# Query tile by query tile: the last attention group's evacuation and the closing steps of the last four tiles

## What is computed

```python
# L1 attention, H = 16 heads of Q/K width 8 and V width 32
Q = _split_heads(x, H)
K = _split_heads(x @ Wk + bk, H)
V = _split_heads(x @ Wv + bv, H)
scores = jnp.einsum('bhqd,bhkd->bhqk', Q, K) + mask      # causal
attn = jax.nn.softmax(scores, axis=-1)
o = jnp.einsum('bhqk,bhkd->bhqd', attn, V)
return x + jax.nn.gelu(o, approximate=False) @ Wf + bf
# L1 feed-forward
h = jax.nn.relu(jnp.einsum('bsd,dw->bsw', x, w1) + b1)
return jnp.einsum('bsw,wd->bsd', h, w2) + b2
# the layers, the last two of six
x = x + _L1_attn_ref(_layernorm(x, axis=-1), ...)
x = x + 0.5 * _L1_ffn_ref(_layernorm(x, axis=-1), ...)
```

## Time and profile before

| | us |
|---|---|
| median of 3 runs | 1076.71 |
| lowest, highest | 1074.05, 1086.48 |
| the profiled execution, its own time | 1089.29 |
| its span | 1087.5 |
| PE busy in it | 920.0 (85%) |
| DVE busy | 713.5 (66%) |
| ACT busy | 513.0 (47%) |
| mean granted PE clock | 0.948 of full speed |

### The profile page before, as it was taken

One profiled execution on the slowest core, in us unless ns is written; L12 is line 12 of the kernel. 1 busy time (PEld: TensorE's weight loads), 2 busy tenths in 40 slices (PEclk: granted clock), 3 DMA queues, 4 the chain that ended last, 5 costly groups with the idle time before them and its releaser, 6 DMA issues.

```text
span 1087.5 us, 19966 instructions
## 1 busy us (share of the span) xinstructions
PE 920.0 (85%) x7332; PEld 459.6 (42%) x7353; DVE 713.5 (66%) x1675; ACT 513.0 (47%) x884; POOL 257.8 (24%) x405
## 2 busy tenths in 40 slices
PE   2788888778888687798889899899899989999986
PEld 1444446565676466444323333233322223332225
DVE  7899953468876666775755588566488757676012
ACT  1133332234444232354565556656556656566772
POOL 1546420045554555421311001112000000000000
PEclk9999998999998887988999899999899999999997
DMA  5300000000000040041002300001500000000000
GB/s 183 67 14 1 1 0 1 1 1 1 1 2 1 1 79 10 2 81 20 23 11 58 54 8 24 2 12 35 74 2 11 12 1 15 7 10 5 12 2 10
DMA packets 30935, 23.20 MB, mean 21 GB/s; under 512 B 9609, under 2 KB 27897, under 8 KB 30840
## 3 DMA queue, kind: packets, MB, share of 16 engines
q1 hardware_dynamic: 29928, 21.39, 9.1%
q10 hardware_dynamic: 912, 0.54, 0.2%
HBM read 17.32 MB, written 4.34 MB: 20 GB/s over the span
## 4 chain that ended last, share of the span: by engine, by line
PE 61%; DVE 16%; ACT 7%; POOL 6%; issue 5%; DMA 3%; SPq 1%; ACTq 0%; DVEq 0%; POOLq 0%
PE psum L1677 11%; PE psum L1692 10%; PE psum L1653 7%; DVE arena L1290 5%; PE psum L1618 5%; PE psum L1565 3%; PE psum L1412 3%; PE psum L1371 2%; ACT arena L967 2%; PE psum L1576 2%; PE psum L1534 2%; PE psum L1422 2%; POOL rs L697 2%; DMA arena<-arena 2%; PE psum L1599 2%
## 5 line engine op out<-in xcount | busy, mean ns | idle before, releaser
L1290 DVE TENSOR_REDUCE arena<-psum 128x2 f32<-128x1024 f32 (+2 forms) x320 | 336.3, 1063 | 146.6 <-PE psum L1618 83.2
L967 ACT ACTIVATE arena<-psum 128x1024 f32<-128x1024 f32 (+3 forms) x320 | 286.7, 898 | 169.3 <-PE psum L1653 95.6
L697 POOL TENSOR_TENSOR rs<-ve,mhalf 128x1 f32<-128x1 f32 x128 | 70.7, 559 | 389.3 <-DVE ve L1084 388.8
L1677 PE MATMUL psum<-arena 128*32 128x512 f32 (+3 forms) x1280 | 153.2, 551 | 1.3 <-ACT arena L967 1.3
L1692 PE MATMUL psum<-arena,ones 128*32 128x512 f32 (+3 forms) x1280 | 153.7, 553 | 0.0
L1618 PE MATMUL psum<-arena 48*128 48x512 bf16 (+3 forms) x640 | 114.2, 358 | 25.9 <-ACT arena L967 13.8
L1653 PE MATMUL psum<-arena 50*128 50x512 bf16 (+3 forms) x640 | 116.8, 361 | 11.6 <-DMA arena<-arena 4.0
L1653 PEld LDWEIGHTS psum<-arena 50*128 50x128 bf16 x640 | 31.1, 93 | 200.8 <-issue 135.1
L936 ACT ACTIVATE rh<-psum,fb 128x128 f32<-128x128 f32 x128 | 36.5, 370 | 60.9 <-PE psum L1565 56.9
L803 POOL TENSOR_TENSOR arena<-arena 128x512 f32<-128x512 f32 x15 | 19.1, 1274 | 188.2 <-DMA arena<-scr_sums 188.2
L1371 PE MATMUL psum<-WguT,xqT 128*128 128x352 f32 x128 | 52.1, 536 | 7.0 <-DVE hb L1115 5.8
(11 more groups left out here) (186 smaller groups left out, 1494.9 us busy)
## 6 DMA issues: line engine op xcount, KB each, us to landing
arena<-scr_parts SPq DMA_DIRECT2D x96, 64.0 KB
arena<-scr_sums SPq DMA_DIRECT2D x60, 64.0 KB, 2.0
scr_parts<-arena SPq DMA_DIRECT2D x12, 256.0 KB, 2.6
arena<-arena SPq DMA_DIRECT2D x124, 2.0 KB, 1.7
X<-in_L_attn_src_dram SPq DMA_DIRECT2D x4, 256.0 KB, 4.9
out_dram<-X SPq DMA_DIRECT2D x16, 64.0 KB, 1.6
arena<-in_c_zsel_dram SPq DMA_DIRECT2D x1, 512.0 KB, 3.8
arena<-in_L_attn_Wk_dram SPq DMA_DIRECT2D x1, 512.0 KB
```

Of the source, the lines that this page charges most:

```text
L697: v.tensor_tensor(rs[:, u, t:t + 1], ve[:, u, t:t + 1], mhalf[:, :], ALU.pow).then_inc(s_rstd[u], 1)
L967: v.activation(pr[:, u % RING, pp, :, 0:CH - off], both(("scores", n))[0][:, :, off:CH], ACT.Exp).then_inc(s_p, 1)
L1290: v.tensor_reduce(MXP[:, j, 2 * pp:2 * pp + 2, m], both(("max", g, pp, j, m))[0][:, :, 0:hi - lo], AX_X, ALU.max).then_inc(s_mxd, 1)
L1677: last = mm(bank(O_BANK)[VD * h:VD * h + VD, off:CH], V[kb // TPC][:, kb % TPC, GH * (g % GPC) + h, :], pr[:, u % RING, h // 2, h % 2, 0:C ...
```

## The change

The last group (g = 15, `LAST`) no longer waits for its last cell. Behind diagonal cell 12+j no later cell adds to the columns of query tile j, so these 128 columns of both banks are final. `take_tile` copies them from bank 6 to `GT` on ACT, and `invert_tile` takes the reciprocal of the sums on DVE straight out of bank 7 into `DN` and multiplies. `take_o`, `take_d` and `invert_last` fall away for this group. Since PE goes on writing into the same two banks, `values` and `sums` of the next diagonal cell wait for the copy and for the reciprocal of the tile before (`s_otl`, `s_dtl`). Behind the cells, `gelu` moves from iteration end+3 to end+1, and the chains of the four tiles start one iteration apart where they stood side by side. The test for the last group in `gather_sums` goes, since it isn't called for it any more.

```diff
+        s_otl, s_dtl = sem("last_o_tile_copied"), sem("last_dn_tile_inverted")
...
                     put(end + 2, "store_inverse", g)
                     put(end + 3, "spread_inverse", g)
                     put(end + NORM_AT, "norm", g)
-                else:
-                    for j in range(TPC):
-                        put(end + 1 + j // 2, "invert_last", g, j)
                 if g % GPC == GPC - 1:
-                    put(end + (3 if last else GELU_AT), "gelu", c)
+                    put(end + (1 if last else GELU_AT), "gelu", c)
                     for j in range(TPC):
                         t = TPC * c + j
-                        put(end + (4 if last else GELU_AT + 1 + j), "wf", t)
-                        first = end + (5 if last else RELU_START + RELU_TILE * j)
+                        put(end + (1 if last else GELU_AT + 1) + j, "wf", t)
+                        first = end + (2 + j if last else RELU_START + RELU_TILE * j)
                         for k, name in enumerate(("f_stats", "d_norm", "d_turn", "d_hidden", "d_out", "d_add")):
                             put(first + k, name, 2 * TILES + t)
             out = [x for k in sorted(slots) if k < 0 for x in slots[k]]
...
                     if 0 < u <= len(CELLS):
                         out.append(("values" if i == 0 else "sums", u - 1))
                         g, kb = CELLS[u - 1]
-                        if kb == TPC * (g // GPC + 1) - 1:
+                        if g + 1 == MGROUPS and kb >= TPC * (CHUNKS - 1):
+                            out.append(("take_tile" if i == 0 else "invert_tile", kb % TPC))
+                        elif kb == TPC * (g // GPC + 1) - 1:
                             out.append(("take_o" if i == 0 else "take_d", g))
                     out += others[cut * i:cut * (i + 1)] + slots.get(2 * u + i, [])
 
...
                     act.wait_ge(s_wf, TPC * (c - 1))
                 v.copy(GT[c % 2][:, g % GPC, :], bank(O_BANK)).then_inc(s_ot, 1)
 
+            def take_tile(j):
+
+                q = slice(P * j, P * j + P)
+                act.wait_ge(s_av, GROUP_U[LAST] + TPC * (CHUNKS - 1) + j + 1)
+                if j == 0:
+                    act.wait_ge(s_wf, TPC * (CHUNKS - 2))
+                v.copy(GT[LAST // GPC % 2][:, LAST % GPC, q], bank(O_BANK)[:, q]).then_inc(s_otl, 1)
+
             def take_d(g):
                 act.wait_ge(s_dn, GROUP_U[g + 1])
                 if g >= 2:
...
                 dve.wait_ge(s_dg[g % 2], 16 * GH * (g // 2 + 1))
                 v.reciprocal(DG[g % 2], DG[g % 2]).then_inc(s_rd, 1)
 
-            def invert_last(g, j):
+            def invert_tile(j):
+
                 q = slice(P * j, P * j + P)
-                r = DN[g % 2][:, q]
-                o = GT[g // GPC % 2][:, g % GPC, q]
-                dve.wait_ge(s_dt, g + 1)
-                dve.wait_ge(s_ot, g + 1)
-                me.wait(me.did(v.reciprocal(r, r)))
+                r, o = DN[LAST % 2][:, q], GT[LAST // GPC % 2][:, LAST % GPC, q]
+                dve.wait_ge(s_dn, GROUP_U[LAST] + TPC * (CHUNKS - 1) + j + 1)
+                if j == 0:
+                    dve.wait_ge(s_on, LAST - 1)
+                v.reciprocal(r, bank(D_BANK)[:, q]).then_inc(s_dtl, 1)
+                dve.wait_ge(s_dtl, j + 1)
+                dve.wait_ge(s_otl, j + 1)
                 v.tensor_tensor(o, o, r, ALU.mult).then_inc(s_onl, 1)
 
             def add_wf(n):
...
                     pe.wait_ge(s_vc, TPC * (c + 1))
                 if kb == 0:
                     B[O_BANK].free(pe)
+                if g == LAST and kb > TPC * (CHUNKS - 1):
+                    pe.wait_ge(s_otl, kb - TPC * (CHUNKS - 1))
                 pe.wait_ge(s_p, GP * (u + 1))
                 for h in range(GH):
                     last = mm(bank(O_BANK)[VD * h:VD * h + VD, off:CH], V[kb // TPC][:, kb % TPC, GH * (g % GPC) + h, :],
...
                 end = kb == TPC * (c + 1) - 1
                 if kb == 0:
                     B[D_BANK].free(pe)
+                if g == LAST and kb > TPC * (CHUNKS - 1):
+                    pe.wait_ge(s_dtl, kb - TPC * (CHUNKS - 1))
                 for h in range(GH):
                     last = mm(bank(D_BANK)[VD * h:VD * h + VD, off:CH], ones1[:, 0:VD],
                               pr[:, u % RING, h // 2, h % 2, 0:CH - off], start=(kb == 0), stop=end,
```

More of the change, by code:

```diff
@@ L357, in build @@
         GROUP_U = [CELLS.index((g, 0)) for g in range(MGROUPS)] + [len(CELLS)]
+        LAST = MGROUPS - 1
         MAXES = [[(g, pp, j, m) for pp in range(GP) for j in range(TPC)
@@ L519, in build @@
         PLAN += causal(PLAN)
-        for kind in sorted({x[0] for x in PLAN} - {"quotients", "max", "invert_last"}):
+        for kind in sorted({x[0] for x in PLAN} - {"quotients", "max"}):
             counts = [x[1] for x in PLAN if x[0] == kind and len(x) == 2]
@@ L657, in gather_sums @@
             def gather_sums(g):
-                if g + 1 < MGROUPS:
-                    sp.wait_ge(s_dt, g + 1)
-                    w = GH * CH // P
-                    for h in range(GH):
-                        sp.dma_start(DG[g % 2][VD * h:VD * h + VD, :],
-                                     DN[g % 2][VD * h:VD * h + 1, :].rearrange("o (p n) -> o p n", n=w)
-                                     ).then_inc(s_dg[g % 2], 16)
+                sp.wait_ge(s_dt, g + 1)
+                w = GH * CH // P
+                for h in range(GH):
+                    sp.dma_start(DG[g % 2][VD * h:VD * h + VD, :],
+                                 DN[g % 2][VD * h:VD * h + 1, :].rearrange("o (p n) -> o p n", n=w)
+                                 ).then_inc(s_dg[g % 2], 16)
             def store_inverse(g):
@@ L1001, in _ @@
                    ff0=lambda g: gelu_ff(g, 0), ff1=lambda g: gelu_ff(g, 1), d_turn=d_copy, d_hidden=d_relu,
-                   e_turn=e_turn, e_k=e_k, e_v=e_v, scores=exponentials, take_o=take_o, take_d=take_d, gelu=gelu,
+                   e_turn=e_turn, e_k=e_k, e_v=e_v, scores=exponentials, take_o=take_o, take_tile=take_tile, take_d=take_d, gelu=gelu,
                    turn_max=max_copy)
@@ L1329, in _ @@
                    e_norm=e_norm, max=take_max, row_max=row_max,
-                   invert=invert, invert_last=invert_last, wf=add_wf)
+                   invert=invert, invert_tile=invert_tile, wf=add_wf)
         @block.tensor
```

## The result

Over 20 runs of each the median went from 1081.17 us (1070.11 to 1092.59) to **1072.85 us** (1064.69 to 1077.95). The ratio is 0.9947 [0.9923, 0.9970], which is 5.7 us faster; over all 20 runs of each the mean fell by 8.3 us, with a standard error of 1.5. The first figure is the smaller one because the ratio leaves out executions more than 1.5% above a kernel's fastest: 5 of 20 of before, none of after. The three differences of the means together are 7.85 +- 0.95 us.

The account below looks back on a forecast made before the run. PE bounds the chain; the last group's tail loses time to two pauses (4.29, 3.08 us) and half clock. Terms 2.2 + 7.0 + 1.3 = 10.5 us, taken as 10 off the 1076.71 median: 1066.7 us, range 1061 to 1074.

Parts of the forecast that it names:

- The likeliest case: Whole kernel: a gain of 8.5 to 11.5 us, the forecast itself, chance 0.50.
- the faster old tail: Rival: the old tail ran at full rate in other executions, so gain 4.7 us, time 1072; chance 0.15.
- within 1%: Whole kernel: outcome less than 1% (10.8 us) either way, chance 0.51, against 0.45 faster and 0.04 slower.
- reciprocal from PSUM with its hand-over: Diagonal cells, DVE: reading sums straight from PSUM costs 0.97 us, as from SBUF; 1.26 as upper bound.
- stall ahead of `sums` of cell 15; 14; 13: Diagonal cells: PE waits for the reciprocal 0.6 us before cell 15, on nobody's path, and not before 14 or 13.
- first projection earlier, counted from cell 12: Pause behind the last cells: second copy, reciprocal and product go, so the first projection starts 2.2 us earlier.
- first projection to first hidden layer: Tail: 11.67 us become 4.65, saving 7.0, of which 2.6 are clock.
- one round: Tail, per tile: 1.38 us waiting for ReLUs, output 0.22 + 0.96, next hidden layer 0.96; 3.52 us.
- The clock in the new tail: Pauses of 0.6 and 1.2 us ahead of the projections keep PE near full rate; half rate there would leave 7.7 gain.
- The rival that took half rate for the rounds: Rounds in the tail: clock falls, a round takes 5.4 us, gain 3.0 or loss 0.7 (1073.7 or 1077.4); chance 0.11.
- The first rival: Old tail's clock elsewhere unknown: full rate gives gain 4.7 (chance 0.15), half-rate outputs too give 14 (0.20).
- the reciprocal: Rival: DVE's reciprocal holds the banks; gain gone at 6.2 us each, over 1% slower at 12; chance 0.04.

Follow-up runs that it names:

- e2: The kernel before with only the banks taken out by query tile, chains still in blocks of four tiles; ratio 0.9940, tail 34.55 us.
- e1: The kernel before, unchanged, profiled a second time; ratio 1.0000 to the runs beside it, tail 37.21 us.
- e7: The changed kernel with each reciprocal of `invert_tile` done twice; tail 32.05 us in one profiled execution.
- e3: The kernel before with only the four tiles' chains one iteration apart, both banks still copied whole; ratio 0.9915, tail 32.16 us.
- e5: The changed kernel again, without edit; ratio 0.9951, tail 29.06 us.
- e6: The changed kernel with next tile's hidden layer ahead of the output, norms later, ACT's copy ahead of the ReLUs; ratio 0.9917, tail 25.45 us.
- e11: The kernel before, unchanged, in its fourth profile; tail 37.20 us.

## Why the prediction was right and wrong

The mechanism of the change was right and the size of its gain was not. The likeliest case was a gain of 8.5 to 11.5 us; the tails showed it (9.3 in the mean), the timed runs did not (5.7 by the ratio, 8.3 by the means). The time of 1072.85 fell in the range of 1061 to 1074. That it came out near the 1072 of the faster old tail is luck: that rival had no half rate in the old tail, and all five executions had some. The most likely outcome by the prediction, "within 1%", holds for the size, 0.5%. But 1% was set as what can't be told from no change, and this change was told from none. Step by step, in the trace of after:

| step | predicted | measured |
|---|---|---|
| reciprocal from PSUM with its hand-over the earlier trace rows | 0.97 | 0.97 |
| stall ahead of `sums` of cell 15; 14; 13 | 0.6; 0; 0 | 0.79; 0.15; 0 |
| first projection earlier, counted from cell 12 | 2.2 | 2.1 |
| first projection to first hidden layer | 4.65 | 4.71 |
| one round | 3.52 | 3.30 |
| hidden layer 0 to the end of the last output | 14.1 | 13.2 |
| tail | 29.8 (1077.0 - 1047.24) | 29.11 |
| gain on the trace of before | 10.5 | 11.15 |

**The diagonal cells.** Right. The copies on ACT, costed at nothing, cost nothing: `values` of cell 13 start 2.59 us behind those of cell 12 with and without them. The 0.15 at cell 14 is most of what the first projection lacks of the predicted 2.2. The table load cost 1.28 us and the gelu followed it at once (1047.74, then 1049.04), as in the earlier trace rows. The drain that the Trainium skill (ScalarE: Activation LUTs, What ACT_TABLE_LOAD costs) puts behind a load isn't in this trace either.

**The tail.** Right in its mechanism. The sum had 2.2 + 7.0 + 1.3; measured are 2.1 + 7.0 + 2.1 (the 1.3 is 1.2 by the prediction's own 15.33 and 14.1). The rounds were costed 0.2 us too long: the wait in them was 1.12 to 1.13 and not the 1.38 of the earlier trace rows. In before, those ReLUs waited for the output layer ahead of them, as the row of 1081.70 says; in after they wait for their own hidden layer. That this is the reason for the shorter wait isn't shown.

**The clock in the new tail.** Right: full rate throughout, with a wait of 1.1 us in every 3.3. The rival that took half rate for the rounds falls: three traces of after have these waits and no swing of the clock. The Trainium skill (TensorE: Matmul & The Clock Gate, A second HAM failure mode: psum-queue depth-cycling) reports of another kernel that short idle times between its groups of matmuls made the clock swing between its levels. The traces of this kernel don't show that.

**The clock in the old tail: the first step that failed.** The sum was made against one execution and its gain taken off the runs, as if each of them had the 17 us at half rate: three projections at 0.87 us more each, and the hidden layers from 1069.84 on at half rate. Of five executions two have that, three have 6.8 us and a tail shorter by 3.2. The first rival said that how fast the old tail ran elsewhere was open. It stood there with two bounds, full rate and slower still; what happens lies between the forecast and the first bound. It belonged in the sum itself. With the tails measured afterwards that sum is 8.0 to 11.2 us, 9.3 in the mean, where the prediction had 10.5 and took 10.

**The base: the second step.** "I take the 10 off the median" took 1076.71, of three runs, for the kernel's time. Twenty runs gave 1081.17, and the 31, 23 and 22 runs beside the experiments 1083.16, 1081.05 and 1081.41. The three runs lay 12.4 us apart, so their median was known far worse than the terms were argued. Both errors point the same way: the base was 4.5 us too low and the gain 1.7 us too large against the medians (10 and not 8.3), and 1066.7 came out 6.15 us below 1072.85.

**The chances.** I set 1% as what a measurement can tell from no change and gave "within 1%" the most, 0.51. That size was read from the spread of single runs (12 us). The interval of 20 runs on each side was +- 0.24%, so a gain of 5.7 us, 0.53%, is told from none. The spread of single runs is not the uncertainty of a comparison of many. With a sum of 8 to 11 us and only 0.15 for rivals that lose most of it (half-rate rounds, the reciprocal), "faster" should have stood first.

**What stays open.** What decides between the two kinds of old tail wasn't tried. The point of the clock's fall goes with the kind in all five executions, but no run moved it; and in e2, with its fall 1.8 us behind the start of the turn, the clock stayed at half for 6.8 us all the same. Whether the 4 us by which the starts of cell 12 differ in the mean (1038.9 in three of after, 1043.1 in five of before) mean anything can't be told with a scatter of 9 us. The instructions ahead of cell 12 are the same.

## What to carry to other kernels

A forecast needs the trace for its terms but several runs for its base: when a term rests on the granted clock, look at more than one execution before it is counted, because pauses of 3 us and more here left half rate for 7 us in one execution and for 17 in the next. Pauses cost twice, once as themselves and once in the rate of what follows; cutting them into several of about 1.1 us returned both parts (5.1 us of waits, 4.2 of rate in the mean). And where a chain of short dependent steps is put in rounds, look at what could stand ahead of the wait: moving the next tile's hidden layer, norm and copy forward took another 3.7 us off a tail of 29 in the one execution that was profiled.

## What the runs showed of the hardware

The clock at the end of before was the surprise. Behind the fourth projection PE stood still, and after some 2.3 us of that the granted clock was already at half (about 1067.4, the second window of before). It then stayed there over 10.2 us, in which PE was busy for 8.22. In e1 the clock fell only when PE had been at work again for 1.5 us, and the same code after the same wait was back at full rate 3.4 us behind that. In e7 a wait of 1.85 us, with waits of 0.74 and 1.06 close ahead of it, was followed by 3.4 us at half rate. In after, a wait of 0.79 and one of 1.10 inside a stretch otherwise busy were not.

A reciprocal of 128x128 out of PSUM is the other number that no row of before had: 0.958 us for each of the four, and 0.947 out of SBUF in before. The group in after, then that in before:

```profile
L1325 DVE RECIPROCAL arena<-psum 128x128 f32<-128x128 f32 x4 | 3.8, 958 | 31.5 <-PE psum L1707 31.5
```

```profile
L1316 DVE RECIPROCAL arena<-arena 128x128 f32<-128x128 f32 x4 | 3.8, 947 | 35.1 <-ACT arena L988 35.1
```

Finally, the stretch ahead of the tail scatters, in part with the clock. In the profiled executions of all kernels here its half-rate time ranges from 75 to 119 us. The shortest (75 in e3) goes with the earliest start of cell 12 (1033.14), the longest (119 in e7) with the latest (1050.15). The clock isn't all of it: five executions with 96 us at half rate there (before, e1, e5, e6, e11) start cell 12 between 1038.20 and 1047.24. Over the 43 timed runs of before with e1, an estimate from each run's span and mean granted clock is that the time grows by about 0.3 us for each us at half rate, as it does between the two kinds of tail (3.2 us for 10.2). So a single profiled execution can be 9 us off another of the same kernel, as much as this whole change.
